# Audio tower: the attend matmuls of the inner key tiles issued in two parts

## The reference

```python
scores = einsum("bhqd,bhkd->bhqk", Q, K) * scale
attn   = softmax(scores, axis=-1)
out    = einsum("bhqk,bhkd->bhqd", attn, V)
```

## Time and profile before

| | |
|---|---|
| median of 3 runs | 2288.55 us |
| the profiled execution's own time | 2287.75 us |
| its span, first to last instruction | 2286.0 us |
| TensorE's mean granted clock | 0.981 of full |
| ScalarE busy | 2128.7 us, 93% |
| TensorE busy | 2074.4 us, 91% |
| VectorE, GpSimd busy | 971.2 us, 390.6 us |

### The profile page before, as it was taken

How to read it: one execution, slowest core, us unless ns; L and a number is a source line. 1 busy time by engine, 2 the same in 40 slices (tenths; PEclk the granted TensorE clock), 3 DMA queues, 4 the chain that set the end, 5 groups by cost and what they waited for, 6 DMA issues and landing times.

```text
span 2286.0 us, 123455 instructions
## 1 busy us (share of the span) xinstructions
PE 2074.4 (91%) x56576; PEld 868.6 (38%) x56576; DVE 971.2 (42%) x2291; ACT 2128.7 (93%) x2346; POOL 390.6 (17%) x637
## 2 busy tenths in 40 slices
PE   4798999899998999989999899989999899998885
PEld 2432444344433344334443344434443344433223
DVE  5344334452445434453345533445244542433115
ACT  2499999999999999999999999999999999998994
POOL 2212102130112201131011310213011220111003
PEclk7899999999999999999999999999999999999998
DMA  2312121222111211221121212122211121122001
GB/s 72 82 38 54 40 61 36 59 53 51 47 50 49 64 44 42 57 66 44 49 56 37 71 41 61 37 59 53 51 48 49 50 54 47 41 60 53 19 10 37
DMA packets 115906, 113.92 MB, mean 50 GB/s; under 512 B 41667, under 2 KB 111862, under 8 KB 115377
## 3 DMA queue, kind: packets, MB, share of 16 engines
q1 hardware_dynamic: 112520, 103.85, 17.9%
q10 hardware_dynamic: 2856, 2.08, 0.4%
HBM read 55.16 MB, written 36.86 MB: 40 GB/s over the span
## 4 chain that ended last, share of the span: by engine, by line
ACT 65%; PE 16%; issue 8%; DVE 3%; SPq 3%; POOL 2%; DMA 1%; DVEq 1%; POOLq 0%; ACTq 0%
ACT prob L592 65%; PE PS L1077 6%; PE PS L1047 4%; PE PS L969 2%; SPq L304 2%; PE PS L999 1%; DMA thin<-Osb 1%; SPq L340 1%; PE PS L949 1%; POOL Hs L450 1%; PE PS L1024 1%; PE PS L984 1%; DVE HL L691 0%; DVE HL L689 0%; DVE z L667 0%
## 5 line engine op out<-in xcount | busy, mean ns | idle before, releaser
L592 ACT ACTIVATE prob<-PS 125x1000 f32<-125x1000 f32 x2304 | 2076.6, 1090 | 72.3 <-PE PS L1047 70.3
L1077 PE MATMUL PS<-prob,Vst 64*17 64x500 f32 (+1 forms) x18432 | 1192.0, 580 | 0.7 <-DVE Hs L758 0.6
L1047 PE MATMUL PS<-QA,KA 64*32 64x500 f16 (+1 forms) x18432 | 935.7, 378 | 121.0 <-ACT prob L592 108.8
L1047 PEld LDWEIGHTS PS<-QA,KA 64*32 64x32 f16 (+1 forms) x18432 | 265.1, 90 | 1084.9 <-ACT prob L592 1054.8
L1077 PEld LDWEIGHTS PS<-prob,Vst 64*17 64x17 f32 (+1 forms) x18432 | 334.6, 93 | 33.8 <-issue 7.5
L458 POOL TENSOR_TENSOR sq<-HL 128x500 bf16<-128x500 f16 x96 | 97.9, 1020 | 960.7 <-DVE HL L691 960.7
L689 DVE TENSOR_SCALAR HL<-PS,b_qk 128x500 f16<-128x500 f32 x90 | 66.5, 739 | 445.7 <-PE PS L969 445.7
L969 PE MATMUL PS<-zT,w_qk 64*32 64x250 f32 x5760 | 236.4, 384 | 20.5 <-DVE HL L691 14.5
L465 POOL TENSOR_TENSOR Y<-Hs,be_ln 125x256 f32<-125x256 f32 x96 | 70.2, 731 | 467.0 <-DVE Hs L758 467.0
L999 PE MATMUL PS<-w_o,oT 64*32 64x128 f32 (+1 forms) x6144 | 125.5, 272 | 17.8 <-DMA oT<-Osb 8.2
L969 PEld LDWEIGHTS PS<-zT,w_qk 64*32 64x32 f32 x5760 | 100.0, 107 | 97.7 <-PE PS L969 32.9
(11 more groups left out here) (88 smaller groups left out, 943.3 us busy)
## 6 DMA issues: line engine op xcount, KB each, us to landing
qk_halves_scratch<-HL SPq DMA_DIRECT2D x96, 250.0 KB, 2.3
QA<-qk_halves_scratch SPq DMA_DIRECT2D x384, 62.5 KB
KA<-qk_halves_scratch SPq DMA_DIRECT2D x380, 62.5 KB
oT<-Osb SPq DMA_DIRECT2D x384, 31.2 KB, 2.3
out<-Y SPq DMA_DIRECT2D x23, 448.0 KB
X<-in_x SPq DMA_DIRECT2D x16, 234.4 KB
thin<-Osb SPq DMA_DIRECT2D x96, 7.8 KB
Den<-thin SPq DMA_DIRECT2D x96, 7.8 KB
```

What stands on the lines that cost most here:

```text
L592: act.activation(prob[0:T, 2 * (w % 6):2 * (w % 6) + 2, :], PS[0:T, 2 * (w % 2):2 * (w % 2) + 2, 0:QC], ACT.Exp, scale=scl)\
L1047: last = pe.matmul(PS[lo:hi, bank, 0:QC], KA[rows, G % NG, h // 2, t * T + lo:t * T + hi], QA[rows, G % NG, h // 2, c * QC:(c + 1) * QC], ...
L1077: last = pe.matmul(PS[lo:lo + HD + 1, bank + r, 0:QC], Vst[rows, b % 2, t, g * HG + j, :], prob[rows, (HG * t + j) % 12, :], start=(t == 0 ...
```

## The change

`attend` is given a third argument, the range of query columns that it treats. The first and the last key tile of a unit are still done in one call over all 500 columns (`WHOLE`), in period 2 of the unit and in period 0 of the next. The ten tiles between them are done in two calls: columns 0 to 399 in the even period in which the whole stood before, and columns 400 to 499 in the odd period behind it, after that period's scores and ahead of its step of `beside`. `s_pv` is raised by the second call.

```diff
-            def attend(n, t):
+            FIRST_PART, SECOND_PART, WHOLE = (0, 400), (400, QC), (0, QC)
+
+            def attend(n, t, part):
                 b, g, bank = n // NU, (n % NU) // NC, 4 + 2 * (n % 2)
-                if t == 0:
+                if t == 0 and part[0] == 0:
...
-                        last = pe.matmul(PS[lo:lo + HD + 1, bank + r, 0:QC], Vst[rows, b % 2, t, g * HG + j, :],
-                                         prob[rows, (HG * t + j) % 12, :], start=(t == 0), stop=(t == NT - 1))
-                last.then_inc(s_pv, 1)
+                        last = pe.matmul(PS[lo:lo + HD + 1, bank + r, part[0]:part[1]], Vst[rows, b % 2, t, g * HG + j, :],
+                                         prob[rows, (HG * t + j) % 12, part[0]:part[1]], start=(t == 0), stop=(t == NT - 1))
+                if part[1] == QC:
+                    last.then_inc(s_pv, 1)
...
                     if k % 2 == 0 and k:
-                        attend(n, k // 2 - 1)
+                        attend(n, k // 2 - 1, FIRST_PART if k > 2 else WHOLE)
+                    elif k > 4:
+                        attend(n, k // 2 - 1, SECOND_PART)
                     elif k == 0 and n > 0:
-                        attend(n - 1, NT - 1)
+                        attend(n - 1, NT - 1, WHOLE)
```

More of the change, by code:

```diff
@@ L1188, in run @@
                 pe.wait_ge(s_free, at(s_free, FREED[LAST]))
-                attend(B * NU - 1, NT - 1)
+                attend(B * NU - 1, NT - 1, WHOLE)
                 for e in range(CT + 1, NT):
```

## The result

The changed kernel takes 2428.64 us (median of 4 runs, 2418.49 to 2431.83) against 2288.58 before (4 runs): a ratio of 1.0608, 95% interval [1.0578, 1.0637], 140 us slower. Slower was forecast, by the mechanism that made most of it; 2350 was forecast too, with 2282 to 2420, and the time lies 9 us above that range. The profiled execution took 2418.49 us with a span of 2416.8, so the traces differ by 130.8 us of span.

The account below looks back on a forecast made before the run. The prediction took ScalarE, busy 93% of the span, as setting the pace, with gains possible only in its waits. It summed 2287.75 + 0 (matmul time) - 4 (levelling) + 67 (instruction fetch) = 2351, said 2350 us, range 2282 to 2420.

Parts of the forecast that it names:

- the fetch theory: Term 3's claim: TensorE gets its instructions at no more than one packet of 256 in a turn.
- The stops: Places where TensorE stands idle in the middle of its program with no semaphore to blame; forecast one every 256 instructions.
- Term 3: Instruction fetch in dense pairs: 3.55 us for 256 instructions where ScalarE's pace asks 2.87; 67 us lost, chance 0.73.
- the turn: Time from TensorE's going on behind a stop until it can begin the next 256-instruction packet, none in store; taken as 3.55.
- the reserve: At each dense stretch's start, ScalarE's and TensorE's queued work covers 0.75 us of late fetch: 80 us over 107 stretches.
- Term 1: Matmul time: attend's second part takes 0.20 us, a dense pair 1.73, under ScalarE's 1.793; hidden, at no cost.
- Term 2: Levelling: scores behind stops in units 4, 5 and 7 no longer come 0.15 us late; 4.2 us won.
- A: Rival: instruction fetch is hidden, asked for early enough or quicker than 3.2 us; 2284 us, chance 0.12.
- B: Rival: levelling behind stops in units 4, 5 and 7 wins more, 7 us in all; 2281 us, chance 0.10.
- C: Rival: attend's second part costs over 0.26 us, its small matmuls waiting for weight loads; 2298 us, chance 0.05.

Follow-up runs that it names:

- cut without move: Changed kernel with both calls, columns 0 to 399 and 400 to 499, in the even period: 2423.57 us, 1.0577 of the kernel before.
- dense: Changed kernel, cut in two only where the odd period has an `out` or `val` step (345 pairs): 2371.44 us, 1.0375 of the kernel before.
- light: Changed kernel, cut in two only where the odd period has neither an `out` nor a `val` step (615 pairs): 2309.26 us, 1.0108 of the kernel before.
- cut in three: Changed kernel with inner key tiles in three parts: columns 0 to 199 and 200 to 399 in the even period, 400 to 499 in the odd: 2753.11 us, 1.2021.
- cut at 250: Changed kernel with the inner key tiles cut at column 250 instead of 400: 2410.33 us, 1.0526 of the kernel before.
- the cut with instructions taken out: Changed kernel with each `out` and `val` step as 8 matmuls over all 128 rows instead of 16 over halves: 2336.84 us, 1.0185.
- full rows in the kernel before: Kernel before with each `out` and `val` step as 8 matmuls over all 128 rows instead of 16 over halves: 2323.89 us, 1.0140.
- both kernels with wide scores: Scores as one matmul of 125 weight columns instead of four with 32: changed kernel 2680.46 us, 1.1693; kernel before 2646.42 us, 1.1541.
- the cut behind stops: Changed kernel, cut only at eight (unit, pair) places in units 4, 5 and 7: 2289.79 us, 1.0011 of the kernel before.

## Why the prediction was right, and where it was not

**Direction and mechanism: right.** Six predictions of the fetch theory that set it apart from a cost of the move, of small matmuls or of each cut came out within their ranges (cut without move, dense, light, cut in three) or close to them (cut at 250, 5 us under; the cut with instructions taken out, expected 2305 to 2335, measured 2336.84). The stops lie on multiples of 256 instructions, and 566 packets were forecast and counted. The four others missed: full rows in the kernel before and both kernels with wide scores, because the edit itself made TensorE slower than the fetch theory allowed for, and the cut behind stops by 0.8 us, with no gain where 4 us less the stops' cost was expected.

**Term 3, its size: this is the step that failed,** in the sentence "The fetch gives them in 3.55". I had 3.92 from an empty queue and took 3.55, because dense stretches before ran at 3.57 a piece without stops. That row didn't show the turn: TensorE asked for no more than 256 in 3.57 there, and the queue covered what was lacking. Once it is empty the turn is 3.85 in the stretch shown of the changed kernel (3.98 on the mean of 68), and 3.58 to 3.87 in the windows with three cuts (3.75 on the mean of 349). Put 3.75 in the prediction's own sum: (3.75 - 2.87) x 216 = 190, less 80, and (3.75 - 3.59) x 180 = 29 for `qk` and `tok` pairs, is 139. The sum becomes 2287.75 - 4 + 139 = 2423; measured were 2428.64. So 0.2 us in one number that is multiplied by some 400 pieces is 72 of the 140 us. This shows how much hangs on the turn, and isn't a measurement of term 3: 3.75 was taken after the result. The changed kernel's own 3.98 in the same sum gives 240 - 80 + 70 = 230, far too much, so the turn alone doesn't put the sum right; the reserve was mis-sized too, the other way.

**The range.** The text had 3.85 and 179 us as the upper end of term 3, 2463, and then a range to 2420. The turn of 3.85 shown is at that end, and the time lies inside those bounds; the range was cut shorter than they made it.

**The reserve of 0.75 for each of 107 stretches** agrees with the runs at most as a sum. With 3.75 it gives 110 us for the dense pairs and 29 for the light ones, where the two kernels with one kind cut have 83 and 21, and the other 37 of 140 come only with both. How turn and reserve share the loss stays open. Likely, light pairs at 3.59 a piece don't refill the queue; and stops of over 0.4 us are found in all twelve units, where I named five.

**Term 1: right.** 0.20 for the second part, by the difference of the two kernels with wide scores, and 0.19 in a row; 0.17 behind a stop. It stayed hidden.

**Term 2: right in the row, wrong in the sum.** The 1.05 becomes 0.88; by the rows behind it a whole gain needs the next pairs cut too, and then the instructions cost more. Whether it would bring 4 us with instructions free can't be told from these runs.

**The rivals.** A and B are out: the fetch isn't hidden. The Trainium skill, "Runtime: NRT & Kernel Launch", section Instruction fetch mechanics, has the cost of an edge as mostly hidden, and these traces don't agree: here an edge is hidden while 256 instructions take longer than one turn, or while the queue in front of TensorE covers the difference. C is out by the cut at 250 and by term 1.

## What to carry to other kernels

Count TensorE's instructions, not only its time: divide the instructions of the densest few microseconds by 256 and compare with the time of one packet's turn, which an engine with "issue" idle in the middle of a group can show. The name isn't enough: the sign is that such gaps lie whole multiples of 256 instructions apart, each about 1.4 us behind the landing of a packet. A float32 matmul is four instructions and a cut of it in two costs four more, whatever its columns. When a row shows a resource keeping pace, it bounds it at the pace that was asked of it, and says nothing about one step more.

## What the runs showed of the hardware

- TensorE's program comes in packets of 256 instructions, and the next packet starts 1.2 us behind TensorE's going on, so that it seems to be asked for only when the one before is begun. Of a turn of 3.85 us, 1.2 pass until the packet starts, 1.1 in the packet, and 1.6 until TensorE goes on (1.4 in the middle over the changed kernel's 68). Two windows of the kernel cut in three have 3.58 and 3.87 on the mean, that is 72 and 66 instructions a microsecond; over its whole trace turns are 3.67 with the other queues quiet and 3.85 with them busy.
- Matmuls with 125 weight columns between ones with 17 or 32 cost 0.14 us at each change of width, and over 128 rows between ones over 64 the wait ahead of them is 0.32 instead of 0.21.
